# A vision tower on one core: most slot results reloaded beside the last expert pairs, and both bias products of a pair side by side

## The reference

```
h = patches(x) @ W.T                               # 64 x 196 x 192
h = layernorm(h + retention_attention(h))          # 12 heads, decay, gate, own layer norm
# slot experts ("soft" mixture): 64 slots, one expert each
xn  = rms_norm(h) * norm_w
log = slots_normalised @ tokens_normalised         # 64 x 196 per image
y   = softmax over tokens (log) applied to xn      # slot inputs, 64 x 192 per image
y   = gelu(fc1[s] . y + fc1_bias[s])               # 768 wide
y   = fc2[s] . y + fc2_bias[s]                     # slot results, 192 wide
out = softmax over slots (log), transposed, applied to y
h = layernorm(h + out)
```

## Time and profile before

| | us |
|---|---|
| median of 3 runs | 1286.35 |
| lowest, highest | 1285.54, 1289.03 |
| the profiled execution | 1285.4 |
| its span, first to last instruction | 1283.7 |

### The profile page before, as it was taken

The page is one execution under the profiler, slowest core; times in us unless marked ns, Lnnn a source line. Parts: engine busy times, 40 slices in busy tenths (PEclk is TensorE's granted clock), DMA queues, the critical chain, the costliest instruction groups (busy, mean ns, idle before and its releaser), DMA issues.

```text
span 1283.7 us, 34970 instructions
## 1 busy us (share of the span) xinstructions
PE 1189.2 (93%) x12938; PEld 956.2 (74%) x12938; DVE 816.2 (64%) x2114; ACT 735.8 (57%) x1677; POOL 571.7 (45%) x878
## 2 busy tenths in 40 slices
PE   5999999999999999999999999999998999997463
PEld 4788888888888888888888888888886555554232
DVE  4677676777777777767777777777673222222797
ACT  5456676776767666777767676666753111110566
POOL 3355455554555554545555455555433000000564
PEclk8999999999999999999999999999999999998555
DMA  4412111111111111111111111121071999994886
GB/s 142 187 49 74 66 53 59 51 50 50 50 50 50 50 66 72 53 54 55 50 50 50 50 50 50 56 81 53 14 265 68 385 419 422 419 393 100 229 261 187
DMA packets 50549, 158.34 MB, mean 123 GB/s; under 512 B 5338, under 2 KB 31312, under 8 KB 38096
## 3 DMA queue, kind: packets, MB, share of 16 engines
q1 hardware_dynamic: 32912, 145.04, 31.0%
q10 hardware_dynamic: 17600, 12.78, 3.2%
HBM read 132.18 MB, written 25.62 MB: 123 GB/s over the span
## 4 chain that ended last, share of the span: by engine, by line
PE 77%; DVE 16%; issue 2%; DMA 1%; ACT 1%; SPq 1%; DVEq 1%; POOL 0%; ACTq 0%; POOLq 0%
PE ps L933 11%; PE ps L934 10%; PE ps L935 10%; DVE p_sb L789 7%; PE ps L993 7%; PE ps L1028 6%; PE ps L1207 5%; PE ps L1224 4%; PE ps L1071 3%; PE ps L976 3%; PE ps L977 3%; PE ps L1011 2%; PE ps L1229 2%; PE ps L1238 2%; DVE res L902 2%; PE ps L1094 2%
## 5 line engine op out<-in xcount | busy, mean ns | idle before, releaser
L412 POOL TENSOR_TENSOR xl<-x_sb,xh 128x392 fp32r<-128x392 f32 x192 | 189.0, 1015 | 86.0 <-DVE gn L764 78.0
L789 DVE TENSOR_TENSOR p_sb<-ps,dec 98x1176 f32<-98x1176 f32 x128 | 176.9, 1382 | 56.0 <-PE ps L993 56.0
L993 PE MATMUL ps<-qm,kT 32*98 32x196 f32 x1536 | 117.0, 343 | 9.6 <-DVE p_sb L789 7.5
L644 ACT ACTIVATE hg<-ps 128x768 f32<-128x768 f32 x32 | 26.0, 812 | 157.2 <-PE ps L1229 157.2
L1028 PE MATMUL ps<-p_sb,vpad 98*32 98x98 f32 x3072 | 112.4, 250 | 1.9 <-DVE p_sb L789 1.9
L1028 PEld LDWEIGHTS ps<-p_sb,vpad 98*32 98x32 f32 x3072 | 84.5, 109 | 35.4 <-issue 24.7
L993 PEld LDWEIGHTS ps<-qm,kT 32*98 32x98 f32 x1536 | 75.2, 158 | 35.1 <-DVE p_sb L789 23.0
L894 DVE COPY y2st<-ps 128x192 f32<-128x192 f32 x32 | 11.4, 358 | 131.4 <-PE ps L1207 131.4
L1253 PE MATMUL ps<-y2b,cbuf 64*98 64x192 f32 x256 | 50.6, 549 | 43.9 <-POOL y2b L512 43.9
L661 ACT ACTIVATE o_sb<-res,nb,rstd 98x192 f32<-98x192 f32 x128 | 59.6, 536 | 51.8 <-DVE nb L917 51.2
L456 POOL TENSOR_TENSOR invn<-nrm,expo 98x4 f32<-98x4 f32 x32 | 32.7, 1021 | 117.7 <-DVE nrm L774 117.4
(11 more groups left out here) (186 smaller groups left out, 3640.9 us busy)
## 6 DMA issues: line engine op xcount, KB each, us to landing
x_sb<-in_xT SPq DMA_DIRECT2D x32, 1176.0 KB, 5.1
w1v<-in_fc SPq DMA_DIRECT2D x32, 1152.0 KB, 7.9
w2v<-in_fc SPq DMA_DIRECT2D x32, 1152.0 KB, 10.5
h_dram<-h SPq DMA_DIRECT2D x32, 294.0 KB
h2r<-h_dram SPq DMA_DIRECT2D x32, 294.0 KB
out<-o_sb ACTq DMA_DIRECT2D x32, 294.0 KB
comb_dram<-cst SPq DMA_DIRECT2D x32, 98.0 KB, 1.7
cbuf<-comb_dram SPq DMA_DIRECT2D x32, 98.0 KB, 3.9
```

Source lines behind the costliest of these rows:

```text
L412: pool.tensor_tensor(xl[:, k], x_sb[:, k], xh[:, k].bitcast(F32), ALU.subtract)\
L789: dve.tensor_tensor(dst, src, rate.unsqueeze(2).to_broadcast([T, PAIRS, 2, TOK]), ALU.mult)\
L993: mm = pe.matmul(ps[0:T, SC_AT + r, mt * TOK:(mt + 1) * TOK].rearrange("p (b n) -> p b n", b=2), kT[rows, g, n], qm[rows, g, :, n], start= ...
```

## The change

Two things change. In the pair stage, PE does the bias products of both halves first and then the products over 128 rows of both halves. At the end of the pair stage, SP no longer waits for all results before it reloads any: when the second product of pair 27 is done and the results of the first 27 pairs (U_SOON) are stored, it issues their part of y2r, 54 of the 64 rows of each half, in four blocks of eight image pairs (eight transfers, semaphore y2r_soon). Behind the last store it issues the other ten rows of each half in two parts, (0, 8) and (8, 32). GpSimd waits for all of the early part and for the first late one before its first y2b, and for the second late part before its loop.

```diff
--- before.py
+++ after.py
@@ -48,7 +48,8 @@
 EARLY = 4
 STAGE_AT = 4 * 24832
 SLOT = 3 * F + 2 * FJ * D
-PARTS = ((0, DEEP), (DEEP, 3 * DEEP), (3 * DEEP, NP))
+U_SOON = 27
+PARTS = ((0, 2 * DEEP), (2 * DEEP, NP))
 Y2 = 3
 assert RING % Y2 == 0
 BANK = 512
@@ -238,7 +239,7 @@
         tr_mm, hgT_rdy, fc2_mm, y2st_rdy = (sem(n) for n in ("tr_mm", "hgT_rdy", "fc2_mm", "y2st_rdy"))
         y2_stored = [sem(f"y2_stored{n}") for n in range(Y2)]
         h2r_loaded = [sem(f"h2r_loaded{n}") for n in range(DEEP)]
-        y2r_loaded = [sem(f"y2r_loaded{n}") for n in range(len(PARTS))]
+        y2r_soon, y2r_loaded = sem("y2r_soon"), [sem(f"y2r_loaded{n}") for n in range(len(PARTS))]
         cbuf_loaded = [sem(f"cbuf_loaded{n}") for n in range(DEEP)]
         y2b_rdy, cmb_mm, res_rdy = (sem(n) for n in ("y2b_rdy", "cmb_mm", "res_rdy"))
         mv3_rdy, rstd3_rdy = sem("mv3_rdy"), sem("rstd3_rdy")
@@ -369,11 +370,21 @@
             for n in range(DEEP):
                 load_comb(n, n)
                 load_h2(n, n)
+
+            def load_y2(u0, u1, p0, p1, there):
+                for a in range(2):
+                    rows = slice(64 * a + 2 * u0, 64 * a + 2 * u1)
+                    sp.dma_start(y2r[rows, p0:p1, :], y2_dram[2 * u0:2 * u1, a, p0:p1, :]).then_inc(there, 16)
+
+            sp.wait_ge(fc2_mm, RING * TURNS - 2)
+            for m in range(Y2):
+                sp.wait_ge(y2_stored[m], 16 * ((U_SOON - m + Y2 - 1) // Y2))
+            for p in range(0, NP, 2 * DEEP):
+                load_y2(0, U_SOON, p, p + 2 * DEEP, y2r_soon)
             for m in range(Y2):
                 sp.wait_ge(y2_stored[m], 16 * ((NU - m + Y2 - 1) // Y2))
             for (p0, p1), there in zip(PARTS, y2r_loaded):
-                for a in range(2):
-                    sp.dma_start(y2r[64 * a:64 * a + 64, p0:p1, :], y2_dram[:, a, p0:p1, :]).then_inc(there, 16)
+                load_y2(U_SOON, NU, p0, p1, there)
             with sp.Fori(0, NP // DEEP - 1) as w:
                 for n in range(DEEP):
                     p = DEEP * w + n
@@ -511,6 +522,7 @@
             def bias(p, n):
                 pool.tensor_tensor(y2b[:, n], y2r[:, p], b2[:, :], ALU.add).then_inc(y2b_rdy, 1)
 
+            pool.wait_ge(y2r_soon, 32 * NP // (2 * DEEP))
             pool.wait_ge(y2r_loaded[0], 32)
             for n in range(DEEP):
                 bias(n, n)
@@ -1219,6 +1231,8 @@
                     f = slice(x * FH, (x + 1) * FH)
                     pe.matmul(ps[:, x, 0:FH], pickb[:, n % 2, x:x + 2].rearrange("p s b -> p (s b)"), bias1[:, f],
                               start=True, stop=False)
+                for x in range(2):
+                    f = slice(x * FH, (x + 1) * FH)
                     for s in range(2):
                         at = 64 * half_of(s, x)
                         pe.matmul(ps[at:at + 64, x, 0:FH], y_u[:, u, s], w1v[n][:, s, f], start=False, stop=False)
```

## The result

| | before | after |
|---|---|---|
| median, us | 1286.35 | 1271.87 |
| lowest, highest of 3 runs | 1285.54, 1289.03 | 1270.35, 1273.06 |
| ratio, 95% interval | 1 | 0.9883 [0.9867, 0.9899] |
| span of the profiled execution | 1283.7 | 1270.1 |

The change saves 14.5 us; forecast were 1271.5 us and a saving of 14.9 against the median (14.5 in the sum itself).

A forecast was written before the change was run, and what follows sets the result against it. PE sets the pair stage's pace with DMA almost full behind it; VectorE bounds the output stage. GpSimd's 7.2 us plus VectorE's 7.3 us gap make 14.5 us off 1286.35: 1271.9, given as 1271.5; range 1266 to 1280.

The forecast's parts named there:

- (a): Pair stage on PE: the second bias product takes 0.19 us instead of 0.37, saving 0.18 us per pair.
- (b): Pair stage on PE: joining the two halves' groups over 128 rows drops one fixed part, 0.15 us per pair.
- Rival B: Pair stage: PE saves little, 0 to 0.18 us per pair, giving 1278.7 or 1274.5 us; chance 0.12.
- The early part at 208 GB/s, ending at 1170.8: End of pair stage: 2.65 MB of y2r start at 1158 behind SP's queue and take 12.8 us.
- Rival C: Early reload runs on part of the engines at 117 GB/s, ending at 1180.7; 1281 us, chance 0.11.
- The last store at 5 us: End of pair stage: the last result's store takes 5 us beside the reload, landing at 1169.1.
- GpSimd 7.2 us earlier: Start of output stage: GpSimd's first y2b starts at 1173.2 instead of 1180.4.
- VectorE's gap of 7.3 us goes: Output stage: VectorE's 7.32 us wait after two steps, for rstd queued behind GpSimd's wait for the last parts, disappears.
- The sum: Whole kernel: 7.2 us from GpSimd's earlier start plus 7.3 from VectorE's gap, 14.5 us saved.
- A: All hidden: early part by 1164, last store in 1.64 us, 17.9 us saved, 1268.4 us; chance 0.16.
- D: Slower: 54 rows spread over 2 engines at 53 GB/s, early part ends at 1208; 1308 us, chance 0.03.
- E: Neither saving shows and the early part merely displaces: about 1286 us; chance 0.05.

The follow-up runs named there:

- e1_bias_only: The kernel before with only the bias products side by side, y2r reloaded as before behind the last store; 1275.03 us, ratio 0.9912.
- e3_u24: The changed kernel with 48 of each 64 rows read early (U_SOON 24) instead of 54; 1270.47 us, ratio 0.9884.
- e13_all_rows: Early part as four transfers over all 128 partitions from expert weights, against eight over 48 of 64 rows (e3_u24), contents wrong; 1269.26 us, one run.
- e2_reload_only: The changed kernel with the bias products back in their old places, so the early reload alone; 1276.99 us, ratio 0.9927.
- e12_u24_one: The changed kernel with 48 rows early and only one image pair's cbuf and h2r preloads ahead of them; 1267.89 us, ratio 0.9851.
- e9: e8 with the last two image pairs' cbuf and h2r preloads put behind the late parts; 1269.26 us, ratio 0.9868.
- e8: e3_u24 with the upper half's early transfers issued on ScalarE's queue after the gelu of pair 30; 1271.95 us, ratio 0.9893.

## Why the prediction was right

Step by step, in its own terms:

- *(a) and (b), 0.33 us per pair.* Measured 0.35 (5.85 less 5.50), the upper bound that was given, and e1_bias_only gives 0.34 from the time alone. The split was right too: 0.18 + 0.19 was forecast for the biases and 0.35 measured, 1.45 for the joined group and 1.44 measured. That the fixed 0.15 us belongs to the change of shape was argued from two groups of the chain; the joined group shows that it goes, and that swapping the column halves costs nothing, but not whether shape or number format is behind it. The bound "a saving over 0.42 would be given back" wasn't reached, and weights landed 18 to 21 us after issue, near the forecast 20, with PE unbroken. Rival B is out.
- *The early part at 208 GB/s, ending at 1170.8.* 219 GB/s on average, ending about 1169.5. The number was right and its reason only in part: 208 was taken over from a transfer on sixteen engines, and here nine carried it. The prediction left open whether the engine or something behind it limits y2r; for sixteen engines e3_u24 and e13_all_rows show that it is the half of the partitions, for the nine at 24 GB/s each both limits lie near each other. Rival C, 117 GB/s, is out. The queue ahead of it ends near the 1158 that was forecast (2.65 MB at 215 GB/s are 12.3 us, back from 1169.5), and SP was free by 1146 as forecast, although four of its issues took 2.5 us each, which the prediction did not see.
- *The last store at 5 us.* It took 6.43. This is the term that was mis-sized, by 1.4 us: between the ends 1.64 and 8.3 the value should have stood nearer the upper one, and the sign that was given, 3 to 6 us, was missed by 0.4.
- *GpSimd 7.2 us earlier.* 5.7: the 1.4 of the store is nearly all of the difference. The first res came at 1177.11 for the 1175.6 that was given as a sign.
- *VectorE's gap of 7.3 us goes.* 7.7 us, from the first res to the third, 0.4 more, since the steps also run closer. e2_reload_only shows it without PE's part (1181.86 to 1187.27, also 5.41), and e1_bias_only keeps it.
- *The sum.* 5.7 + 7.7 = 13.4, for 7.2 + 7.3 = 14.5; the median's saving is 14.5 us, so about one microsecond of the agreement is luck between the profiled execution and the runs. The last step from 1271.9 to 1271.5 had no reason, and 1271.87 was measured.
- *Rivals.* A (all hidden, 1268.4) was wrong for this kernel, but it is what e12_u24_one reaches: 1267.9 with the store at 1.65. D (2 engines, 1308) was wrong for 54 rows and right in its cost: 46 rows give 1299.9. E is out, since both savings show.

## What to carry to other kernels

Two edits that each save on the same path don't add up when one brings the end of the stage into the transfers that the other has moved there: time both halves alone, and look at the landing time of the last small store between them. Of a transfer, look at the number of rows (its greatest divisor up to 16 shows in the DMA share) and at how many partitions they lie in; moving the cut from 54 to 48 rows changed little, and from 48 to 46 cost 29 us. Products of one shape belong together, since each of the two seams that went had cost 0.15 to 0.2 us here.

## What the runs showed of the hardware beyond that

- Nine DMA engines reached nearly the rate of sixteen (219 for 233 GB/s from 1158 to 1166) on rows in one half of the partitions, 24 GB/s for an engine; over all 128 partitions sixteen reached 391 to 398.
- Transfers into both halves from two queues at once, SP with GpSimd or with ScalarE, moved 202 and 213 GB/s on average (184 to 253 in single stretches), no more than one queue with both (233).
- Four issues in a row on SP took 2.5 us each instead of 0.4, in the changed kernel and in e1_bias_only, while weights were landing 18 to 21 us after issue: the engine that issues is held, not only the transfer.
- The preloads of cbuf and h2r move 235 to 264 GB/s with nearly all engines busy (the kernel before, 1152 to 1156, all weights landed), where the weights move 420: four image pairs of them cost the queue some 6 us.
- A store of 128 short rows that takes 1.64 us alone takes 4.5 to 8.8 beside a bulk reload in other queues, and 3.5 and 6.8 where part of the reload stands in its own (e9, e8).
